# Attention inside a three-part block: the causal mask of the exponentials applied by GpSimd, head by head, instead of by a mask product on TensorE

## The reference, cut to what matters

```python
q, k, v = (heads(Wq, bq), heads(Wk, bk), heads(Wv, bv))      # 16 heads of 16
q = _apply_rope(q, cos, sin)
k = _apply_rope(k, cos, sin)
att = jnp.einsum('bhqd,bhkd->bhqk', q, k) * (1.0 / np.sqrt(D))
att = jnp.where(causal[None, None], att, NEG_BIG)
att = jax.nn.softmax(att, axis=-1)
y = jnp.einsum('bhqk,bhkd->bhqd', att, v)
```

## Time and profile before

| what | us |
|---|---|
| median of 3 runs (2717.07 to 2720.41) | 2720.24 |
| the profiled execution's own time | 2707.74 |
| its span, first to last instruction | 2706.0 |
| mean granted TensorE clock | 0.916 of full speed |

### The profile page before, as it was taken

The page is one execution under the profiler, slowest core; times in us unless marked ns, Lnnn a source line. Parts: engine busy times, 40 slices in busy tenths (PEclk is TensorE's granted clock), DMA queues, the critical chain, the costliest instruction groups (busy, mean ns, idle before and its releaser), DMA issues. The chain is left out here.

```text
span 2706.0 us, 43185 instructions
## 1 busy us (share of the span) xinstructions
PE 2227.9 (82%) x14740; PEld 1451.9 (54%) x14740; DVE 1699.0 (63%) x5181; ACT 1218.6 (45%) x2442; POOL 966.9 (36%) x1344
## 2 busy tenths in 40 slices
PE   6659999935699999999999999999962664899997
PEld 6658888834334444444444444443322664788886
DVE  7435555433477877877878878877733663555552
ACT  1224444411056665665666665666750212344443
POOL 3723434326423333333333333330002564333442
PEclk9999999965589999999999999999986775999999
DMA  9552223021524434435344344344315424323220
GB/s 341 187 197 96 88 71 104 29 73 58 132 64 110 117 84 111 112 86 130 87 110 114 86 97 111 80 105 99 80 60 124 144 69 165 126 71 100 77 71 22
DMA packets 185131, 283.21 MB, mean 105 GB/s; under 512 B 14392, under 2 KB 147704, under 8 KB 176720
## 3 DMA queue, kind: packets, MB, share of 16 engines
q1 hardware_dynamic: 170576, 247.08, 34.0%
q0 software_dynamic: 14336, 33.38, 3.5%
HBM read 153.99 MB, written 126.88 MB: 104 GB/s over the span
## 5 line engine op out<-in xcount | busy, mean ns | idle before, releaser
L1646 ACT ACTIVATE at_probs<-at_score_ps 128x512 f32<-128x512 f32 (+3 forms) x1536 | 692.9, 497 | 451.6 <-PE at_score_ps L1763 312.6
L1525 DVE CUSTOM_DVE_ANT_0 at_junk<-at_max_ps,at_causal 128x128 f32<-128x128 f32 (+3 forms) x1024 | 485.5, 484 | 128.2 <-PE at_max_ps L1749 126.2
L1749 PE MATMUL at_max_ps<-at_k,at_q 96*128 96x512 bf16 (+3 forms) x1536 | 494.1, 341 | 43.1 <-DVE at_peak L1525 30.7
L1760 PE MATMUL at_score_ps<-at_q,at_k 99*128 99x512 bf16 (+3 forms) x1536 | 499.3, 332 | 10.7 <-DMA at_v<-v_rows 4.4
L1528 DVE TENSOR_REDUCE at_peak<-at_max_ps 128x1 f32<-128x512 f32 x512 | 352.4, 688 | 118.2 <-PE at_max_ps L1749 114.9
L1037 DVE TENSOR_TENSOR f_hid_lo<-f_hid,f_hid_hi 128x512 fp32r<-128x512 f32 x256 | 177.5, 693 | 322.8 <-ACT f_hid_hi L1061 322.2
L1749 PEld LDWEIGHTS at_max_ps<-at_k,at_q 96*128 96x128 bf16 x1536 | 144.6, 98 | 398.0 <-DVE at_peak L1525 192.0
L1058 ACT ACTIVATE f_hid<-f_hid_ps 128x512 f32<-128x512 f32 x256 | 153.3, 599 | 413.7 <-PE f_hid_ps L1084 413.5
L1773 PE MATMUL at_o_ps<-at_probs,at_v 128*32 128x512 f32 (+3 forms) x3072 | 337.8, 512 | 1.2 <-ACT at_probs L1646 0.7
L1099 PE MATMUL f_y_ps<-f_w_hi,f_hid_hi 128*128 128x256 f32 x1024 | 292.7, 286 | 47.4 <-DVE f_xe L1015 28.9
L1099 PE MATMUL f_y_ps<-f_w_hi,f_hid_lo 128*128 128x256 f32 x1024 | 291.4, 285 | 0.0
(11 more groups left out here) (175 smaller groups left out, 3631.0 us busy)
## 6 DMA issues: line engine op xcount, KB each, us to landing
f_w_raw<-in_w SPq DMA_DIRECT2D x32, 1024.0 KB, 7.6
qk<-at_parts SPq DMA_DIRECT2D x32, 768.0 KB, 4.2
expert_in<-r_zeros SPq DMA_DIRECT2D x16, 1040.0 KB, 11.3
f_xe<-expert_in SPq DMA_DIRECT2D x32, 520.0 KB, 7.3
v_rows<-at_v_outs SPq DMA_DIRECT2D x32, 512.0 KB, 6.2
at_v<-v_rows SPq DMA_DIRECT2D x32, 512.0 KB, 10.4
o_rows<-at_o_out SPq DMA_DIRECT2D x64, 256.0 KB, 2.0
at_q<-qk SPq DMA_DIRECT2D x32, 384.0 KB, 7.6
```

What stands on the lines that cost most here:

```text
L1525: v.tensor_tensor_reduce(junk[bank(k, r)][:, 0:w], src, causal[:, HALF - w:HALF], 1.0, LEAST, ALU.add, ALU.max, out).then_inc(max_used, 1)
L1646: a.activation(probs[t % 2][:, h, c0:c0 + w], score_ps[(GH * t + h) % BANKS][:, 0:w], ACT.Exp, scale=float(SCALE)).then_inc(exp_done, 1)
L1749: te.matmul(max_ps[bank(u, r)][:, 0:w], q[u][0:ROWS, h, i * P:(i + 1) * P], kk[u][0:ROWS, h, k0:k0 + w], start=True, stop=True).then_inc(m ...
L1760: last = te.matmul(out[:, 0:w], kk[u][:, h, j * P:(j + 1) * P], q[u][:, h, hf * HALF + c0:hf * HALF + c0 + w], start=True, stop=not diagonal)
```

## The change

The mask product and its constant `hide` go. After the exponentials of a diagonal step and head, POOL sets the hidden triangle of the 128 x 128 block of `probs` to zero in place with one `affine_select`, and a semaphore `masked` counts steps. `times_v` of a diagonal step waits for `masked` in place of the exponentials and stands at c = 3, no longer at c = 2. POOL does `mask(g, t)` first in each step.

```diff
+            def mask(g, t):
+
+                c0, _, diagonal = columns(STEPS[t])
+                for h in range(GH if diagonal else 0):
+                    pool.wait_ge(exp_done, GH * (NS * g + t) + h + 1 + BANKS)
+                    block = probs[t % 2][:, h, c0:c0 + P]
+                    last = p.affine_select(block, block, [[1, P]], ALU.is_ge, 0.0, base=0, channel_multiplier=-1)
+                if diagonal:
+                    last.then_inc(masked, 1)
...
                 for t in range(NS):
+                    mask(g, t)
                     if finish:
                         if t <= 1:
                             rope(n - 1, 1, t + 1)
...
-                last = te.matmul(out[:, 0:w], kk[u][:, h, j * P:(j + 1) * P],
-                                 q[u][:, h, hf * HALF + c0:hf * HALF + c0 + w], start=True, stop=not diagonal)
+                te.matmul(out[:, 0:w], kk[u][:, h, j * P:(j + 1) * P], q[u][:, h, hf * HALF + c0:hf * HALF + c0 + w],
+                          start=True, stop=True).then_inc(score_ready, 1)
+
+            def times_v(g, u, t):
+                c0, w, diagonal = columns(STEPS[t])
+                hf, j = STEPS[t]
                 if diagonal:
-                    last = te.matmul(out[:, 0:P], sh.ident_bf[:], hide_bf[:], start=False, stop=True)
-                last.then_inc(score_ready, 1)
-
-            def times_v(g, u, t):
-                c0, w, _ = columns(STEPS[t])
-                hf, j = STEPS[t]
-                pe.wait_ge(exp_done, GH * (NS * g + t + 1) + BANKS)
+                    pe.wait_ge(masked, masks_before(g, t) + 1)
+                else:
+                    pe.wait_ge(exp_done, GH * (NS * g + t + 1) + BANKS)
...
-                        if c == 2:
+                        if c == (3 if columns(STEPS[t])[2] else 2):
                             times_v(g, k, t)
```

More of the change, by code:

```diff
@@ L1152, in attention_block @@
         causal = sb("causal", [P, HALF], F32)
-        hide = sb("hide", [P, P], F32)
-        hide_bf = sb("hide_bf", [P, P], BF16)
         junk = [sb(f"junk{k}", [P, HALF], F32) for k in range(BANKS)]
@@ L1217, in attention_block @@
         exp_done = sem("exp_done")
+        masked = sem("masked")
         pv_done = sem("pv_done")
@@ L1258, in bank, with masks_before @@
             return place(k, r) % BANKS
+        def masks_before(g, t):
+            diagonals = [columns(step)[2] for step in STEPS]
+            return sum(diagonals) * g + sum(diagonals[:t])
         def peaks_in_ps(k, r):
@@ L1316, in _ @@
             sp.dma_start(causal[:], dr["causal"]).then_inc(c_loaded, 16)
-            sp.dma_start(hide[:], dr["hide"]).then_inc(c_loaded, 16)
             load_x(1)
@@ L1395, in _ @@
             invert_std(0)
-            pool.wait_ge(c_loaded, 16 * 11)
+            pool.wait_ge(c_loaded, 16 * 10)
             for n in range(LEAD - 1):
@@ L1556, in _ @@
                 v.memset(v_out[s][:, :, :, D:VW], 1.0)
-            dve.wait_ge(c_loaded, 16 * 11)
-            v.tensor_copy(hide_bf[:], hide[:])
+            dve.wait_ge(c_loaded, 16 * 10)
             dve.wait_ge(w_hi_ready, 1)
@@ L1650, in _ @@
             act.sem_inc(o_copied, 1)
-            act.wait_ge(c_loaded, 16 * 11)
+            act.wait_ge(c_loaded, 16 * 10)
             a.copy(w_hi[:], w_raw).then_inc(w_hi_ready, 1)
@@ L1752, in scores @@
             def scores(g, u, t, h):
-                c0, w, diagonal = columns(STEPS[t])
+                c0, w, _ = columns(STEPS[t])
                 hf, j = STEPS[t]
@@ L1924, in shape_constants @@
         "causal": causal,
-        "hide": np.ascontiguousarray(causal[:, HALF - P:].T),
     }
```

## The result

The changed kernel takes 2805.5 us (four runs, 2805.1 to 2808.4) against 2720.0: a ratio of 1.0319, with a 95% interval of 1.0301 to 1.0337. It is 85 us slower where 60 were forecast. The forecast's side and its own range (2740 to 2820) hold; two of the numbers behind it do not.

The account below looks back on a forecast made before the run. DVE was taken to bound each group's first part and PE the second; 42 us (groups with preparation) + 8 (late groups) + 10 (clock) = 60 on 2720 gave 2780 us, own range 2740 to 2820, whole range 2690 to 2890.

Parts of the forecast that it names:

- The stage view: In one attention group, DVE's ring reductions bound steps 1 to 5 (15.54 of 15.70 us busy); PE bounds the later part.
- The products taken from PE: Of 32 mask products per group, only 12, in steps 7, 8 and next step 0, save time: 0.7 us per group.
- The price of a select: One 128 x 128 affine_select on POOL: 0.44 us, counted as 0.42 each in a run of four.
- rival 1: POOL quick enough: at 0.28 us or less per select DVE's backlog hides all; 2682 to 2700 us, chance 0.31.
- The cover: DVE's queued work, lasting until T + 10.7 (T: start of the group's closing L1742), hides part of POOL's lateness, leaving 2.3 us.
- T + 11.6: Forecast start of times_v of step 3 after the group's closing L1742, against T + 7.8 before.
- groups with preparation: The 26 groups where POOL also has rope: + 2.3 - 0.7 = + 1.6 us each, 42 us in all.
- The chain of steps 1 to 3: After mask(0), POOL's queue of rope 1.29 and 1.27 us and three masks of 1.68 us, delaying times_v up to step 3.
- The clock: Stalls at step 0 invite more falls of PE's clock, 1.45 us each: 10 us, bounds - 16 to + 60.
- late groups: The last five groups, where POOL has no rope: + 2.2 less 0.7, + 1.5 us each, 8 us in all.
- The shared port: DVE and POOL operations blocking one another: taken as zero, up to 1.6 us per group higher by the skill's rule.
- Steps 5 to 8 cost nothing: Selects there, 6.7 us of POOL per group, wait behind exponentials that come anyway: costed at nothing.

Follow-up runs that it names:

- sixth kernel: Kernel before the change, with only times_v of the diagonal steps moved from c = 2 to c = 3: ratio 0.9964 to the kernel before.
- eleventh: Neither mask products nor selects, causal mask of the exponentials left out, times_v at c = 3 as in the changed kernel: ratio 0.9979 to the kernel before.
- third kernel: Changed kernel with a second affine_select ahead of each select in steps 1, 2 and 3, 3.0 us more POOL per group: ratio 1.0896 to the kernel before.
- seventh kernel: Changed kernel with the last score product ahead of times_v of step 0 repeated 34 times as filler: 2761.7 us, ratio 1.0178 to the kernel before.
- fourth kernel: Neither mask products nor selects, causal mask left out, times_v at c = 2 as in the kernel before: ratio 0.9994 to the kernel before.
- eighth kernel: Changed kernel with DVE's normalize moved from step 1, c = 2, to step 0, c = 2: ratio 1.0307 to the kernel before.
- fifth kernel: Kernel before with POOL masking steps 5 to 8 only (times_v there at c = 3), product kept in steps 0 to 3: ratio 0.9972 to the kernel before.

## Why the prediction came out as it did

**The stage view was right.** DVE bounds the first part, PE the second. The products taken from PE are worth 0.58 us per group (39.73 against 40.31), 0.7 predicted (a sum that has the four products of step 0 on both sides of its split).

**The price of a select was wrong**, 0.42 us taken in a run of four against 0.25 (1.02 for four; the mean of one row is 296 ns). By the prediction's own rule, under 0.28 us POOL is quick enough and the change wins (rival 1). It lost all the same, so that the forecast had the right side is in part luck: with the right price its own sum would have said faster.

**The cover was wrong, and that is why.** The prediction added POOL's chain up to `times_v` of step 3 and set DVE's backlog there (work until T + 10.7) against all of it. But the waits aren't one wait at the end. The first is at step 0, and there DVE has no backlog: it was idle even before. PE's 1.88 us become 2.59 us of idle DVE, ahead of a stretch in which DVE has almost no slack to win them back. The sum of T + 11.6 for `times_v` of step 3 was met (1338.74 - 1327.47 = 11.3) for another reason, 2.0 of it from step 0 and the rest from the place at c = 3, with the 0.74 us wait for ACT that the sixth kernel also has. Two errors cancelled, and that is luck: 42 us were predicted for the groups with preparation and 36 measured.

**The chain of steps 1 to 3** is hidden as POOL stands now (`times_v` of step 1 to that of step 8 takes 23.66 us in the changed kernel, 23.62 in the sixth and 23.59 in the eleventh, which have no selects), and stops being hidden with 3 us more in it (third kernel).

**The clock was named and priced too low**: 10 us, 33 measured (seventh kernel). The groups with preparation were about right, 15. What was missed is the late groups, where nothing but the stall was counted, 8 us, and 24.6 measured: there every stall brings the clock down, and the filler alone gives back 12.5 of it (176.5 in place of 189.0). The second thing missed lies in the removal: of 0.58 us x 31 = 18 us saved on PE the attention keeps 7, and the rest is given back through the clock (fourth kernel).

**The shared port** was costed at zero, and at this load that held (eighth kernel). The one select of 0.44 us that it took as the most a DVE operation waits was too little: one pair took 4 us in the third kernel. Run back to back, POOL's instructions leave no gap. The Trainium skill, SBUF — State Buffer, section Who interferes with whom, lets the loser wait for the whole instruction of the other; here it waited for a run of them (2.11 us across two).

**Steps 5 to 8 cost nothing**: right, shown by the fifth kernel. **What would show it**: of the signs named, the 2 us at step 0, `times_v` of step 3 near T + 11.6, a POOL without idle time up to step 3 (in the group shown), the unchanged steps 9 to 11 and a mean period of about 43 us (42.9) came. The select over 0.32 us did not, and of the waits at steps 1 to 3 PE shows only one at step 2, of 0.5 us, in 10 of groups 1 to 25.

## What to carry to other kernels

When work goes to an engine with room on the average, find the instruction of its queue that the first consumer will stand behind, and ask what the others have queued at that moment; cover counted at the end of a chain does not help at its start. The same four selects, 1.0 us in all, make the attention 80 us longer behind one DMA issue than ahead of it. Take work from an engine only in the stretch where it is the bound: elsewhere it was free here, and with it TensorE's clock fell less often. The version that follows from both leaves the product in steps 0 to 3 and gives POOL the steps 5 to 8 (0.9972, and 0.9941 with `times_v` at c = 3 everywhere, a place that is worth 0.9964 by itself).

## What the runs showed of the hardware

- Less work for PE made its clock fall more often: 12 falls before, 23 without the mask products (mean over the stretch 0.98 and 0.96). Moving `times_v` by one place, with no work removed, brought the 12 to one.
- Idle time of PE followed by the lower clock cost as much again as the idle time in the late groups: 34.0 us (groups 27 to 29) with filler products in the stall, 36.3 to 37.5 without, 31.7 to 32.1 before.
- An affine_select of 128 x 128 f32 takes 296 ns, and 0.25 us in a run. That is under the 435 ns that a tensor_tensor would take and far under a tensor_scalar's 790, both interpolated from the earlier trace rows and so estimates.
- A DVE tensor_scalar of two columns took 2.11 us beside two POOL instructions without a gap between them, against 0.15 for one of the same size just after it.
